# Graph layer with a selective-state scan: B rows by DMA broadcast, two banks as a ring for B and C, the next tile's gcn product in each tile's last step

## The chip, the cores and the metric

One core of a Trainium2 chip runs the whole program. The metric is the device time of one launch in microseconds (us), as the median over repeated runs; lower is better. The engines are named as in the profile: PE (TensorE, matrix products), DVE (VectorE), ACT (ScalarE), POOL (GpSimd), SP (the queue that only issues DMAs).

## What is computed

Two layers over a graph of 4096 nodes with 128 features. The first computes two branches `relu(...)` of `adj @ x` and `adj @ x2`, merges them, adds x and normalises each row. The second is the one that the change touches:

```
h = relu(adj @ x @ gcn_w + gcn_b); h = layernorm(h) * ln_g + ln_b
xc, z = split(h @ w_in); u = silu(causal_conv4(xc))
dt, B, C = split(u @ w_xp); dt = softplus(dt @ w_dt + b_dt)       # B, C: 16 values for each of 4096 steps
for t in 0..4095: s[d, n] = exp(dt[t, d] * A[d, n]) * s[d, n] + dt[t, d] * u[t, d] * B[t, n]
                  y[t, d] = sum_n s[d, n] * C[t, n]
out = layernorm(x + ((y + u * D_skip) * silu(z)) @ w_out)
```

with 256 channels d and 16 states n.

## The kernel before, in words

The first part of the program (up to about 480 us) is the first layer; it also writes the transposed matrix to DRAM (`adjT`). It isn't touched. The second part works on 8 tiles of 512 time steps. Each engine runs a function `window(b, ...)` for tile b, with one pass of a loop over steps n = 0..15 (plus one or two at its end) for the 16 states. What an engine does in a step is written out by hand, with the table `AT` (which step holds which piece), `PLAN` and `CONV` (how many products of 512 columns PE does in a step), and semaphores between engines.

For state n, with the channels on 128 partitions in 2 halves of 512 steps:

- PE spreads row n of B over all partitions: a product of `bc` with a selector column, into PSUM bank 6 (`spread_B`, line 1117). All 16 rows of B go through this one bank, so each waits until the one before it is consumed. The order is `SPREADS` (1, 0, 3, 2, ...), two steps ahead (`AHEAD`), each at the end of a step after the step's other work.
- For even n, DVE multiplies that bank with `dtu` into `dBuV` (line 887). For odd n, ACT copies the bank to SBUF (`copy_B`, line 655, tile `b_sb`), and POOL multiplies there into `dBuP` (line 480), not before DVE has scanned state n - 3.
- ACT computes `dA` (line 671). DVE scans (line 901, `hs`), one step later.
- PE spreads row n of C (`spread_C`, line 1127), at the end of step n + 1, into bank 5, or bank 4 for n = 1, 3, 5; each waits for the product before it in its bank. DVE multiplies `hs` with it into `pr` (line 908), in step n + 2. PE adds the product to y by 8 turning products (`sum_state`, line 1131), in step n + 3; those of states 14 and 15 (`LATE`) come in step 0 of the next window.

In between, window b does the front of tile b + 1 (`front_*`: gcn product on PE, line 1064; relu on ACT, line 590; statistics `front_g` on DVE, line 839; inverse deviation on POOL, line 450; convolution, z, B, C and dt products on PE; softplus on ACT, DVE line 857 and POOL lines 457, 462, 465), the tail of tile b - 1 (`tail_*`: gate, line 863; output product; statistics, line 869; POOL lines 470 and 472; `tail_norm` on ACT, line 713, in step 14), and for tile b + 2 the 32 blocks of `adj @ x` (`adj_blocks`, line 1052), which sum in bank 7.

These blocks read chunks of 4 blocks each. SP loads a chunk (1024 KB) from `adjT` into one of 4 buffers `adjc` (line 328). In SP's window stands in this order: the chunks 0 to 5 of tile b + 2, the store of tile b - 1's output (line 338), which waits for `tail_norm`, then chunks 6 and 7:

```
                load_res(b, par)
                if adj_:
                    load_adj(b + 2, range(0, CHUNKS - 2))
                if tail:
                    store(b - 1)
                if adj_:
                    load_adj(b + 2, range(CHUNKS - 2, CHUNKS))
```

The gcn product of tile b + 1 is PE's in step 0 of window b, after the sums of states 14 and 15, and ACT's copy of bank 7 for it (`front_ax`, line 585) in step 0 too. Windows 2 to 5 are a loop of two passes.

## Time and profile before

| | us |
|---|---|
| median of 3 runs | 1243.48 (1239.97 to 1245.7) |
| the profiled execution | 1238.24 |
| its span | 1236.7 |
| PE busy / DVE busy in the span | 1042.8 / 1056.5 |
| ACT busy / POOL busy | 543.7 / 325.3 |

The span is the time from the first to the last recorded instruction of the profiled execution; its own time stands 1.5 us above it. Busy time counts every record in full, so an engine that starts an instruction before the last one's record has ended (PE does, DVE a little) is less loaded than it looks. In the rows, `[0.61 <-PE bank L1117]` behind an instruction is its engine's idle time ahead of it and what ended that. State and step numbers are not in the rows: they follow from the order in the code.

### The profile page before, as it was taken

Reading aid. Unit: us, or ns where it says so; the run is one execution under the profiler, and the core shown is the slowest. Engines: PE = TensorE matmul, PEld = TensorE weight load, DVE = VectorE, ACT = ScalarE, POOL = GpSimd, SP = SyncE. Lnnn points to the kernel's source line nnn. Section 1 sums busy time; section 2 is a strip of 40 time slices with the busy share of each in tenths; the row PEclk is TensorE's granted clock in tenths of the full one; section 3 lists DMA queues with packets and bytes.
Section 4 is the critical chain, followed back from the end, with each engine's and each line's share of the span. In section 5 each row is a group of like instructions: output and inputs, shape, how many; then the busy total and the mean of one; then the engine's idle time right before and its main releaser. Section 6 shows DMA issues by size and latency. Waiting matters only on the chain. (4 is left out here: it accounts for less than half of the span.)

```text
span 1236.7 us, 13710 instructions
## 1 busy us (share of the span) xinstructions
PE 1042.8 (84%) x4306; PEld 709.1 (57%) x4306; DVE 1056.5 (85%) x864; ACT 543.7 (44%) x970; POOL 325.3 (26%) x208
## 2 busy tenths in 40 slices
PE   2789999999999999999888888888898888785555
PEld 1567677777777774445455555555455455453444
DVE  5899999999999996337878988978988879899994
ACT  2333333343333322145635546546457266455441
POOL 5100000101000011002262442622723624536330
PEclk9899999999999999999989999989999899896766
DMA  9999999999999998551321250520610511000000
GB/s 254 241 208 307 339 308 342 317 329 321 326 325 317 339 300 149 206 212 69 111 102 68 94 196 1 191 98 1 221 69 0 221 68 65 20 1 18 0 9 9
DMA packets 181948, 209.41 MB, mean 169 GB/s; under 512 B 7968, under 2 KB 163680, under 8 KB 167568
## 3 DMA queue, kind: packets, MB, share of 16 engines
q1 hardware_dynamic: 107008, 165.69, 41.8%
q10 hardware_dynamic: 71808, 35.66, 13.2%
q0 software_dynamic: 3088, 7.54, 2.2%
q8 instruction: 19, 0.31, 0.1%
q14 instruction: 25, 0.20, 0.1%
HBM read 145.94 MB, written 62.91 MB: 169 GB/s over the span
## 5 line engine op out<-in xcount | busy, mean ns | idle before, releaser
L760 DVE STREAM_TRANSPOSE at<-rows 128x1024 f32<-128x1024 f32 x136 | 267.3, 2006 | 26.4 <-DMA rows<-in_adj 16.0
L965 PE MATMUL yT<-ah,xh 128*128 128x512 f32 x512 | 214.4, 419 | 53.4 <-DVE al L768 53.4
L480 POOL TENSOR_TENSOR dBuP<-dtu,b_sb 128x1024 f32<-128x1024 f32 x64 | 165.9, 2592 | 268.7 <-DVE hs L901 211.8
L521 ACT ACTIVATE ah<-at 128x2048 fp32r<-128x2048 f32 x64 | 122.4, 1913 | 240.6 <-PE yT L965 229.4
L1052 PE MATMUL bank<-adjc,xm 128*128 128x512 f32 x448 | 219.0, 624 | 4.7 <-DMA adjc<-adjT 3.8
L965 PE MATMUL yT<-ah,xl 128*128 128x512 f32 x512 | 202.0, 395 | 0.0
L965 PE MATMUL yT<-al,xh 128*128 128x512 f32 x512 | 201.9, 394 | 0.0
L671 ACT ACTIVATE dA<-dt,A_sb 128x512 f32<-128x512 f32 x256 | 169.9, 715 | 47.4 <-POOL dt L462 45.2
L901 DVE TENSOR_TENSOR_SCAN hs<-dA,zero,dBuP 128x1026 f32<-128x1026 f32 x64 | 167.2, 2613 | 5.7 <-issue 4.5
L1131 PE MATMUL yT<-ident,pr 128*128 128x128 f32 x1024 | 152.0, 299 | 18.9 <-DVE pr L908 18.6
L908 DVE TENSOR_TENSOR pr<-hs,bank 128x1024 f32<-128x1024 f32 x128 | 153.0, 1196 | 9.7 <-PE bank L1127 9.7
L901 DVE TENSOR_TENSOR_SCAN hs<-dA,zero,dBuV 128x1026 f32<-128x1026 f32 x64 | 158.6, 2478 | 1.4 <-DVE dBuV L887 0.9
L1131 PEld LDWEIGHTS yT<-ident,pr 128*128 128x128 f32 x1024 | 134.7, 156 | 39.3 <-DVE pr L908 28.1
L965 PEld LDWEIGHTS yT<-ah,xh 128*128 128x128 f32 x512 | 97.6, 191 | 88.4 <-DVE al L768 64.9
L768 DVE TENSOR_TENSOR al<-at,ah 128x2048 fp32r<-128x2048 f32 x64 | 144.4, 2257 | 0.2
L1052 PEld LDWEIGHTS bank<-adjc,xm 128*128 128x128 f32 x448 | 84.6, 200 | 84.3 <-issue 77.3
L1127 PE MATMUL bank<-bc,sel 128*128 128x512 f32 x128 | 60.6, 473 | 77.6 <-DVE pr L908 77.5
L887 DVE TENSOR_TENSOR dBuV<-dtu,bank 128x1024 f32<-128x1024 f32 x64 | 78.0, 1218 | 50.1 <-PE bank L1117 47.3
L965 PEld LDWEIGHTS yT<-ah,xl 128*128 128x128 f32 x512 | 97.6, 191 | 23.8 <-issue 5.0
L965 PEld LDWEIGHTS yT<-al,xh 128*128 128x128 f32 x512 | 97.4, 190 | 21.3
L655 ACT ACTIVATE b_sb<-bank 128x512 f32<-128x512 f32 x64 | 38.0, 593 | 137.2 <-PE bank L1117 137.2
L1117 PE MATMUL bank<-bc,sel 128*128 128x512 f32 x128 | 90.2, 705 | 6.3 <-ACT b_sb L655 3.2
(148 smaller groups left out, 1048.5 us busy)
## 6 DMA issues: line engine op xcount, KB each, us to landing
adjT<-at SPq DMA_DIRECT2D x56, 1024.0 KB, 8.0
adjc<-adjT SPq DMA_DIRECT2D x56, 1024.0 KB, 5.1
rows<-in_adj SPq DMA_DIRECT2D x152, 256.0 KB, 8.6
rows<-in_adj ACTq DMA_DIRECT2D x136, 256.0 KB, 8.7
xm<-in_x SPq DMA_DIRECT2D x4, 512.0 KB, 16.2
xs<-in_L_gnn_x SPq DMA_DIRECT2D x4, 512.0 KB, 15.1
res<-in_x POOLq DMA_DIRECT2D x8, 256.0 KB, 7.5
mid<-xn POOLq DMA_DIRECT2D x8, 256.0 KB, 6.5
```

Of the source, the lines that this page charges most:

```text
L480: nc.gpsimd.tensor_tensor(dBu(n, par)[:, :, 1:], dtu[par][:, :, :], b_sb[pool_slot(n, par)][:, :].unsqueeze(1).to_broadcast([P, H, TILE]), ...
L521: nc.scalar.activation(ah[c % 2][:, :], at[c % 2][:, :, :].rearrange("p m t -> p (m t)"), ACT.Copy)\
L671: nc.scalar.activation(dA[n % NDA][:, h, 1:], dt_[par][:, h, :], ACT.Exp, scale=A_sb[:, h, n:n + 1]).then_inc(dA_ready, 1)
L760: last = nc.vector.transpose(dst.rearrange("p m (g i) -> p g m i", i=32), src.rearrange("p g (i m) -> p g m i", i=32))
L768: nc.vector.tensor_tensor(al[c % 2][:, :], at[c % 2][:, :, :].rearrange("p m t -> p (m t)"), ah[c % 2][:, :], ALU.subtract).then_inc(chunk ...
L887: nc.vector.tensor_tensor(dBuV[dve_slot(n, par)][:, :, 1:], dtu[par][:, :, :], BB[:, :].unsqueeze(1).to_broadcast([P, H, TILE]), ALU.mult)\
L901: nc.vector.tensor_tensor_scan(flat[0], flat[1], flat[2], zero[:, :], ALU.mult, ALU.add)\
L908: nc.vector.tensor_tensor(pr[k % NPR][:, :, :], hs[k % NHS][:, :, 1:], CC[k][:, :].unsqueeze(1).to_broadcast([P, H, TILE]), ALU.mult)\
L965: last = mm(acc[k][:, :], w[:, b, :], v[c % 2][:, cols], start=(b == 0 and j == 0), stop=(b == KB - 1 and j == 2))
L1052: last = mm(accB[:, :], xm[:, b, :], adjc[c % NADJ][:, m, :], start=(b == 0), stop=(b == KB - 1))
L1117: mm(BB[:, :], sel[:, n:n + 1].to_broadcast([P, P]), bc[par][:, :], start=True, stop=True).then_inc(B_spread, 1)
L1131: m = mm(yT[:, DI * q + P * h:DI * q + P * h + P], src[:, h, P * q:P * q + P], ident[:, :], is_transpose=True, start=first and h == 0 and ...
```

## The change

It does three things and moves a few others along.

1. The rows of B for the odd states (POOL's) no longer pass through PE's product and ACT's copy. After `bc` is made, ACT copies the 16 rows of B from PSUM to a small tile `b_rows`, and stores that to DRAM (`b_dram`, 32 KB). Two states at a time, it then issues a DMA which reads two rows and writes them to all 128 partitions (`load_B`, 512 KB, tiles `b_sb`): four such loads for a tile, in ACT's steps 14 (for the next tile), 2, 5 and 9. PE's dt product now also waits for `b_rows`, since it overwrites the bank.
2. Banks 5 and 6 form a ring. The 8 rows of B for even states and the 12 rows of C that aren't in bank 4 (now C of states 0, 2, 4, 6) take the two banks in turn, in the order of their use; each waits for the one two places before it. The row of B for state n + 1 is spread first thing in step n (n odd), row 0 of the next tile at the end of step 16.
3. The gcn product of tile b + 2 comes in the last step (16) of window b on PE, between the sum of state 13 and the spread of C for state 15; ACT's copy for it comes in step 15, the relu in step 0 of the next window. `PLAN` puts the 32 blocks on other steps.

SP's order, POOL's and DVE's are as before.

```diff
-          pe_z=7, pe_dbc=8, pe_dt=10, pe_turn=2, pe_out=9, act_B=-1, act_g=1, act_start=1, act_skip=2, act_y=4)
+          pe_z=7, pe_dbc=8, pe_dt=10, pe_turn=2, pe_out=9, act_b0=14, act_b1=2, act_b2=5, act_b3=9, act_ax=15, act_g=0, act_start=1, act_skip=2, act_y=4)
...
-PLAN = (1, 4, 3, 2, 0, 0, 1, 1, 1, 2, 0, 3, 3, 3, 4, 4)
-C_IN_O = (1, 3, 5)
+PLAN = (2, 4, 4, 1, 1, 0, 2, 1, 2, 1, 1, 3, 3, 2, 3, 2)
+C_IN_O = (0, 2, 4, 6)
...
+        ring = [it for n in range(S + 2) for it in (("B", n), ("C", n - 2))
+                if (it[0] == "B" and n < S and n not in POOL_B) or (it[0] == "C" and n >= 2 and n - 2 not in C_IN_O)]
+        def spread_bank(kind, n):
+            return bank[4] if kind == "C" and n in C_IN_O else bank[5 + ring.index((kind, n)) % 2]
...
                 nc.scalar.activation(bc[par][:, :], M0[:, :], ACT.Copy).then_inc(bcdt_high, 1)
+                nc.scalar.activation(b_rows[:, :], M0[0:S, :], ACT.Copy).then_inc(b_rows_ready, 1)
+                act.wait_ge(b_rows_ready, a + 1)
+                act.dma_start(b_dram[S * par:S * par + S, :], b_rows[:, :]).then_inc(b_stored, 16)
...
-            def copy_B(b, k, par):
-                act.wait_ge(B_spread, S * b + SPREADS.index(k) + 1)
-                wait(act, dBu_by_pool, NPB * b + nB(k) - 1)
-                nc.scalar.activation(b_sb[(nB(k) + NPB * par) % 2][:, :], BB[:, :], ACT.Copy).then_inc(B_copied, 1)
+            def load_B(b, par, pair):
+                if pair == 0:
+                    act.wait_ge(b_stored, 16 * (b + 1))
+                wait(act, dBu_by_pool, NPB * b + 2 * pair - 2)
+                rows_ = b_dram[S * par:S * par + S, :].rearrange("(k two) t -> two k t", two=2)[1]
+                act.dma_start(b_sb[pair % 2][:, :, :], rows_[2 * pair:2 * pair + 2, :].partition_broadcast(P))\
+                    .then_inc(b_in[pair % 2], 16)
...
+                    if n in (AT['act_b1'], AT['act_b2'], AT['act_b3']):
+                        load_B(b, par, 1 + (AT['act_b1'], AT['act_b2'], AT['act_b3']).index(n))
+                    if adj_ and n == AT['act_ax']:
+                        front_ax(b + 2)
                     if front:
-                        if n == (0 if tail else 1):
+                        if n == 1 and not tail:
                             front_ax(b + 1)
...
+                        if n == AT['act_b0']:
+                            load_B(b + 1, 1 - par, 0)
...
             def front_dtp(a, par):
                 pe.wait_ge(bcdt_low, a + 1)
+                pe.wait_ge(b_rows_ready, a + 1)
...
+            def bank_free(b, kind, n):
+                i = ring.index((kind, n))
+                (k, m), bb = (ring[i - 2], b) if i >= 2 else (ring[i - 2], b - 1)
+                if k == "B":
+                    wait(pe, dBu_by_dve, NVB * bb + m - nB(m) + 1)
+                else:
+                    wait(pe, C_multiplied, S * bb + m + 1)
...
             def window(b, par, tail, front, adj_):
                 for n in range(S + 1):
+                    if n % 2 and n + 1 < S:
+                        spread_B(b, n + 1, par)
                     if tail and n == 0:
                         for k in LATE:
                             sum_state(b - 1, k)
-                    if front and n == 0:
+                    if front and not tail and n == 0:
                         front_gcn(b + 1)
...
-                    if n + AHEAD < S:
-                        spread_B(b, n + AHEAD, par)
-                    elif front and n < S:
-                        spread_B(b + 1, n + AHEAD - S, 1 - par)
+                    if adj_ and n == S:
+                        front_gcn(b + 2)
                     if n > 0:
                         spread_C(b, n - 1, par)
+                    if front and n == S:
+                        spread_B(b + 1, 0, 1 - par)
```

Two places on PE show how the order moves. The first is where the blocks of chunk 6 begin (buffer `adjc2`, semaphore `adjT_in2`). Before, from the spread of C for state 11 (end of step 12) to the first block of chunk 6 in step 14; `pr2` and `pr3` hold the products of states 10 and 11:

```order
L1127 MATMUL bank5<-bc1,sel 128x512 [waits C_multiplied]
L1131 MATMUL yT<-ident,pr2 128x128 [waits C_multiplied]
L1131 MATMUL yT<-ident,pr2 128x128 x7
L1052 MATMUL bank7<-adjc1,xm 128x512 x3
L1114 REGISTER_ALU
L1117 MATMUL bank6<-bc1,sel 128x512 [waits B_copied]
L1122 REGISTER_ALU
L1127 MATMUL bank5<-bc1,sel 128x512 [waits C_multiplied]
L1131 MATMUL yT<-ident,pr3 128x128 [waits C_multiplied]
L1131 MATMUL yT<-ident,pr3 128x128 x7
L1052 MATMUL bank7<-adjc2,xm 128x512 [waits adjT_in2]
```

After, step 12 from the sum of state 9 (`pr1`), the spread of C for state 11 (into bank 5) and the start of step 13, with the spread of B for state 14:

```order
L1150 MATMUL yT<-ident,pr1 128x128 [waits C_multiplied]
L1150 MATMUL yT<-ident,pr1 128x128 x7
L1068 MATMUL bank7<-adjc1,xm 128x512 x2
L1068 MATMUL bank7<-adjc2,xm 128x512 [waits adjT_in2]
L35 REGISTER_ALU
L1146 MATMUL bank5<-bc1,sel 128x512 [waits dBu_by_dve]
L35 REGISTER_ALU
L1137 MATMUL bank6<-bc1,sel 128x512 [waits C_multiplied]
L1150 MATMUL yT<-ident,pr2 128x128 [waits C_multiplied]
```

The first block of chunk 6 now stands in step 12, ahead of the spread of C for state 11; before it stood two steps later, behind that spread and the next.

The second place is the end of a window. Before, from the spread of C for state 15 into the next window; `pr2` and `pr3` are states 14 and 15:

```order
L1127 MATMUL bank5<-bc1,sel 128x512 [waits C_multiplied]
L1234 REGISTER_ALU
L1234 COMPARE_AND_BRANCH
L1131 MATMUL yT<-ident,pr2 128x128 [waits C_multiplied]
L1131 MATMUL yT<-ident,pr2 128x128 x7
L1131 MATMUL yT<-ident,pr3 128x128 [waits C_multiplied]
L1131 MATMUL yT<-ident,pr3 128x128 x7
L1064 MATMUL bank2<-gcn_w_sb,axT 128x128 [waits sp_abs_relu,ax1_ready]
L1065 MATMUL bank2<-gcn_b_sb,ones 128x128
```

After, step 16 from the end of state 13's sum (`pr1`) to the spread of B for state 0 of the next tile (into bank 5):

```order
L1150 MATMUL yT<-ident,pr1 128x128 x7
L1080 MATMUL bank2<-gcn_w_sb,axT 128x128 [waits sp_abs_relu,ax1_ready]
L1081 MATMUL bank2<-gcn_b_sb,ones 128x128
L1080 MATMUL bank2<-gcn_w_sb,axT 128x128
L1081 MATMUL bank2<-gcn_b_sb,ones 128x128
L1080 MATMUL bank2<-gcn_w_sb,axT 128x128
L1081 MATMUL bank2<-gcn_b_sb,ones 128x128
L1080 MATMUL bank2<-gcn_w_sb,axT 128x128
L1081 MATMUL bank2<-gcn_b_sb,ones 128x128
L1146 MATMUL bank6<-bc1,sel 128x512 [waits C_multiplied]
L35 REGISTER_ALU [waits bcdt_low]
L1137 MATMUL bank5<-bc0,sel 128x512 [waits C_multiplied]
```

The 8 gcn products have moved from behind the sums of states 14 and 15 to ahead of the spread of C for state 15.

## Rows read from the trace of the kernel before

**Rows 1.** DVE's waits, 544 to 638 us (tile 0): waited for, us, times, longest.

```profile
DVE stats L839 <- ACT g L590: 13.6, 1, 13.6
DVE dBuV L887 <- PE bank L1117: 7.5, 4, 2.6
```

**Rows 2.** The same, 638 to 1068 us (tiles 1 to 5).

```profile
DVE dBuV L887 <- PE bank L1117: 35.2, 25, 3.3
DVE stats L839 <- ACT g L590: 8.8, 4, 2.7
DVE pr L908 <- PE bank L1127: 7.1, 9, 1.6
```

**Rows 3.** The same, 1068 to 1221 us (tiles 6 and 7).

```profile
DVE dBuV L887 <- PE bank L1117: 4.6, 4, 1.7
DVE pr L908 <- PE bank L1127: 1.8, 2, 0.9
DVE stats L839 <- ACT g L590: 1.4, 1, 1.4
```

**Rows 4.** PE: stretch, length, busy us, granted clock (1.00 is 2.4 GHz), DMA share, GB/s.

```profile
638.00:1068.00 430.00, 371.86 (x1590) 0.97 0.26 94
```

**Rows 5.** DVE's timeline in tile 2: start, us, instruction [idle before <-what ended it].

```profile
717.14 4.39 DVE L901 TENSOR_TENSOR_SCAN hs<-dA,zero,dBuP 128x1026 f32<-128x1026 f32 x1 [1.13 <-issue]
...
723.53 1.22 DVE L908 TENSOR_TENSOR pr<-hs,bank 128x1024 f32<-128x1024 f32 x1 [0.89 <-PE bank L1127]
...
734.51 1.22 DVE L887 TENSOR_TENSOR dBuV<-dtu,bank 128x1024 f32<-128x1024 f32 x1 [1.49 <-PE bank L1117]
```

**Rows 6.** POOL's timeline in tile 2.

```profile
733.29 2.38 POOL L480 TENSOR_TENSOR dBuP<-dtu,b_sb 128x1024 f32<-128x1024 f32 x1
741.45 2.40 POOL L480 TENSOR_TENSOR dBuP<-dtu,b_sb 128x1024 f32<-128x1024 f32 x1 [5.78 <-DVE hs L901]
```

**Rows 7.** DVE's timeline in tile 7: two scans, the second behind a `dBuV` without a wait.

```profile
1149.85 2.35 DVE L901 TENSOR_TENSOR_SCAN hs<-dA,zero,dBuV 128x1026 f32<-128x1026 f32 x1
...
1154.37 2.50 DVE L901 TENSOR_TENSOR_SCAN hs<-dA,zero,dBuP 128x1026 f32<-128x1026 f32 x1
```

**Rows 8.** All engines' timeline, 779 to 803 us (tile 2, steps 11 to 17).

```profile
787.77 0.88 SPq L328 DMA_DIRECT2D adjc<-adjT  x2
...
790.66 1.19 DVE L908 TENSOR_TENSOR pr<-hs,bank 128x1024 f32<-128x1024 f32 x1
...
792.24 1.03 PE L1131 MATMUL yT<-ident,pr 128*128 128x128 f32 x8
...
793.34 3.70 PE L1052 MATMUL bank<-adjc,xm 128*128 128x512 f32 x8
...
796.28 3.28 DVE L901 TENSOR_TENSOR_SCAN hs<-dA,zero,dBuV 128x1026 f32<-128x1026 f32 x1
```

**Rows 9.** PE's timeline at the start of tile 3: first of 8 gcn products, next block.

```profile
811.11 0.39 PE L1064 MATMUL bank<-gcn_w_sb,axT 128*128 128x128 f32 x2
...
814.33 1.97 PE L1052 MATMUL bank<-adjc,xm 128*128 128x512 f32 x2
```

**Rows 10.** PE's timeline where chunk 6 came late, then the clock behind it (stretch as in rows 4).

```profile
881.79 5.40 PE L1052 MATMUL bank<-adjc,xm 128*128 128x512 f32 x8 [1.86 <-DMA adjc<-adjT]
...
883.80:887.20 3.40, 3.40 (x7) 0.65 0.93 378
```

**Rows 11.** ACT's copies of B's rows in all, then its DMA issues in the first part.

```profile
L655 ACT ACTIVATE b_sb<-bank 128x512 f32<-128x512 f32 x64 | 38.0, 593 | 137.2 <-PE bank L1117 137.2
...
196.25 0.46 ACTq L281 DMA_DIRECT2D rows<-in_adj  x1
```

**Rows 12.** DMA issues: KB each, median us to landing; then `adjc` min/median/max.

```profile
xm<-in_x SPq DMA_DIRECT2D x4, 512.0 KB, 16.2
out<-o_n SPq DMA_DIRECT2D x8, 256.0 KB, 2.6
...
DMA to landing us min/median/max: 4.7/5.1/11.8
```

More of the change, by code:

```diff
@@ L159, in gnn_mamba @@
         y = sb("y", [P, H, TILE], F32, B)
-        b_sb = [sb(f"b_sb{k}", [P, TILE], F32, B) for k in range(2)]
+        b_sb = [sb(f"b_sb{k}", [P, 2, TILE], F32, B) for k in range(2)]
+        b_rows = sb("b_rows", [S, TILE], F32, B)
         o_n = sb("o_n", [P, RG, D], F32, B)
@@ L172, in gnn_mamba @@
         accB, M0, M1 = bank[7], bank[2], bank[3]
-        BB = bank[6]
-        CC = [bank[4] if n in C_IN_O else bank[5] for n in range(S)]
         O = bank[4][:, :].rearrange("p (g d) -> p g d", g=RG)
@@ L232, in gnn_mamba @@
         dtu_ready = sem("dtu_ready")
-        B_spread, C_spread, B_copied = sem("B_spread"), sem("C_spread"), sem("B_copied")
+        B_spread, C_spread = sem("B_spread"), sem("C_spread")
+        b_rows_ready, b_stored = sem("b_rows_ready"), sem("b_stored")
+        b_in = [sem(f"b_in{k}") for k in range(2)]
         dA_ready, start_set = sem("dA_ready"), sem("start_set")
@@ L882, in window @@
                     if n < S and n not in POOL_B:
[L883 removed]
+                        dve.wait_ge(B_spread, NVB * b + n - nB(n) + 1)
                         if n == 0:
@@ L1105, in front_dtp, with spread_B @@
                     mm(m[:, :], w_dtl[:, P * h:P * h + P], bc[par][:, :], start=False, stop=True).then_inc(dt_product, 1)
-            def spread_B(b, p, par):
-                n = SPREADS[p]
-                if p == 0:
-                    pe.wait_ge(bcdt_low, b + 1)
-                k, bb = (SPREADS[p - 1], b) if p else (SPREADS[-1], b - 1)
-                if not (isinstance(bb, int) and bb < 0):
-                    if k in POOL_B:
-                        pe.wait_ge(B_copied, NPB * bb + nB(k) + 1)
-                    else:
-                        pe.wait_ge(dBu_by_dve, NVB * bb + k - nB(k) + 1)
-                mm(BB[:, :], sel[:, n:n + 1].to_broadcast([P, P]), bc[par][:, :], start=True, stop=True).then_inc(B_spread, 1)
+            def bank_free(b, kind, n):
[5 more added lines that the diff above has]
+                    wait(pe, C_multiplied, S * bb + m + 1)
+            def spread_B(b, n, par):
+                if n == 0:
+                    pe.wait_ge(bcdt_low, b + 1)
+                bank_free(b, "B", n)
+                mm(spread_bank("B", n)[:, :], sel[:, n:n + 1].to_broadcast([P, P]), bc[par][:, :], start=True, stop=True).then_inc(B_spread, 1)
             def spread_C(b, n, par):
-                before = [k for k in range(n) if (k in C_IN_O) == (n in C_IN_O)]
-                if before:
-                    pe.wait_ge(C_multiplied, S * b + before[-1] + 1)
-                elif n in C_IN_O:
+                if n not in C_IN_O:
+                    bank_free(b, "C", n)
+                elif n == C_IN_O[0]:
                     wait(pe, o_normed, RG * (b - 1))
                 else:
-                    wait(pe, C_multiplied, S * b)
-                mm(CC[n][:, :], sel[:, S + n:S + n + 1].to_broadcast([P, P]), bc[par][:, :], start=True, stop=True).then_inc(C_spread, 1)
+                    pe.wait_ge(C_multiplied, S * b + C_IN_O[C_IN_O.index(n) - 1] + 1)
+                mm(spread_bank("C", n)[:, :], sel[:, S + n:S + n + 1].to_broadcast([P, P]), bc[par][:, :], start=True, stop=True).then_inc(C_spread, 1)
             def add_turned(src, h, first=False, last=False):
@@ L1226, in _ @@
             pe.wait_ge(selectors_ready, 4)
-            for p in range(AHEAD):
-                if p == 1:
-                    fill(7)
-                spread_B(0, p, 0)
+            spread_B(0, 0, 0)
+            fill(7)
             fill(8)
```

34 lines of the change are left out of this document (15 added, 19 removed).

## The prediction

> **What bounds the kernel now.** I read the waits of DVE first, because in the scan part it is the engine that everything else serves: 16 scans, 16 products with C and 8 with B in each tile, in a fixed order. In tile 0 it waits 13.6 us once for g, the input of the next tile's statistics, and 7.5 us for rows of B [rows 1]. In tiles 1 to 5 it waits 35.2 us for rows of B in 25 waits, five a tile, 8.8 us for g and 7.1 us for rows of C [rows 2]; in tiles 6 and 7, 4.6, 1.4 and 1.8 us [rows 3]. The waits for B are PE's order, not its load: PE is busy 372 of 430 us in tiles 1 to 5 at a granted clock of 0.97 [rows 4], but a row of B is issued at the end of a step, behind up to four blocks, and an even state's row can't be issued before the odd row ahead of it has been copied out of the one bank. So DVE's order plus these waits sets the time.
>
> The second thing to see is a loss that is no wait. A scan takes 2.35 us, but 4.39 us when POOL's product for `dtu` has just begun [rows 5, 7]. Both read two tensors from SBUF, and one stands until the other is through. At a tile's end POOL's softplus chain costs DVE 1.13 us of idle time ahead of scan 15, 2.04 us in it [rows 5] and 0.93 us in scan 14 (3.28 against 2.35) [rows 7, 8]: 4.1 us a tile.
>
> **What the change takes away.** B's row for each even state is now issued first thing in a step and needs only a bank that was used two items before, so I take all its waits off: 7.5 + 35.2 + 4.6 = 47.3 us [rows 1 to 3]. With the gcn product a step earlier, g is there before DVE asks: 8.8 + 1.4 = 10.2 us. Tile 0's 13.6 us stay, since that product hangs on the 32 blocks ahead of window 0, which aren't moved. Row 15 of C no longer waits for the product of state 14: 1.8 us in tiles 6 and 7, which have no gcn product at their end. Together 59.3 us.
>
> **What it gives back.**
>
> (a) The waits for B were cover. POOL's product for an odd state starts when DVE's scan ends and takes 2.4 us; DVE fills 2.25 us with a product with C and one with B, then wants to scan. Where no wait stands there now, that scan takes 2.50 us and not 2.35 [rows 7]. About 30 scans get this: 4.5 us.
>
> (b) POOL's product for state 3 comes after its work on the statistics and runs from 733.29 to 735.67 [rows 6]. DVE, without its 1.49 us wait [rows 5], would be at scan 1 1.5 us earlier, and stand until 735.6. So that wait only changes its name: 7 x 1.5 = 10.5 us.
>
> (c) The table for PE's blocks. Blocks 24 to 27 are chunk 6. They began in step 14 and now begin in step 12, ahead of the spread of C for state 11. But SP still issues that load behind the output's store, which waits for ACT's step 14; nothing of that chain is moved. In tile 2 the load was issued at 787.77, and PE began on it at 793.34, the moment it was there [rows 8]. DVE takes C for state 11 at 790.66. Now C comes one block (0.9 us) and one spread (0.4 us) behind the landing: at 794.6, a wait of 4.0 us, and I take 4.3 us, since part of it runs at the lower clock. While DVE stands, POOL works through its chain, so that of the 4.1 us above only some 1.3 us are left; PE, late by then, costs DVE some 0.6 us in steps 13 to 15. Net 4.3 - 2.8 + 0.6 = 2.1 us a tile, in the five tiles which have both a store and a chunk 6 (1 to 5): 10.5 us.
>
> (d) Step 16. After DVE's product of state 13, PE adds it (1.03 us [rows 8]), does 8 gcn products (814.33 - 811.11 = 3.2 us [rows 9]) and spreads C for 15 (0.4 us): 4.6 us. DVE has a scan and a product to do meanwhile, 2.35 + 1.19 = 3.5 us [rows 7, 8]. It waits at least 1.1 us, up to 3.0 if PE is a block or two behind; I take 2.0, where 0.89 was [rows 5]. Six tiles: 6.6 us.
>
> (e) ACT loses 64 copies of 0.59 us [rows 11] and gets per tile one copy and five DMA issues, of 0.46 us each by the one row for it [rows 11]. It isn't waited for now, so both are worth nothing, but 0.3 us ahead of window 0, where the copy and the issue stand in the chain. Without ACT's slack the issues would cost 2.3 us a tile.
>
> (f) The broadcast loads are in no row. From below: a 256 KB transfer lands in 2.6 us; from above: 512 KB took 16.2 us under full queues [rows 12]. The tightest is the load in ACT's step 2, which serves the product at 741.45 [rows 6]; ACT is at step 2 near scan 14 of the tile before, over 20 us ahead. I take nothing; the cover is POOL's distance.
>
> Given back: 4.5 + 10.5 + 10.5 + 6.6 + 0.3 = 32.4 us. Net 59.3 - 32.4 = 27 us. From the profiled execution, 1238.2, that gives 1211; that execution is 5 us below the median of the runs, 1243.5, and from the median the forecast is **1216 us**.
>
> **A rule against it.** ACT's queue is empty in this part before, so no row has two queues loading at once. In ACT's step 14 the first broadcast of the next tile is issued a few us ahead of chunk 6. The Trainium skill (DMA: Bandwidth & Descriptors, Issuing engines are not separate DMA queues) says that DMAs from different engines run on the same 16 DMA engines and interleave. By that rule the sum would be some 12 us smaller, 1229 us; by the rows alone it is 1216. It is the second rival, priced from rows there.
>
> **The rivals.**
>
> *The wait for chunk 6 is hidden (0.17).* If the load were there by 789.3, (c) falls away and the time is 1206. For it: DVE could lag for other reasons. Against: the load's issue hangs on DVE's own steps, so it moves along with DVE.
>
> *The broadcast delays chunk 6 (0.15).* 512 KB is half of a chunk, which takes 5.1 us to land [rows 12], so up to 2.5 us more, five times: 12.5 us, 1229. For it: the two are issued within 3 us. Against: the first should be nearly through when the second begins.
>
> *C for states 0 and 1 comes late (0.07).* Steps 1 and 2 have four blocks each (3.7 us) ahead of those spreads; at the lower clock they'd take twice that. 1.5 us in seven tiles: 1227. This is also the way in which the early rows of B would bring nothing: the wait moves on to C.
>
> *PE stays at half clock to the end of the tile (0.08).* PE comes to chunk 6 two steps earlier than now, where it comes just as the load lands, so it waits some 9 us. Behind a wait of 1.86 us eight instructions took 5.40 us, not 3.70, with the clock at 0.65 of its full rate over the next 3.4 us [rows 8, 10], that is at 1.2 GHz for most of it. If it stayed there over steps 13 to 16, four sums and seven blocks would take 4 x 1.03 + 7 x 0.9 = 10 us longer; half of it would reach DVE: 5 x 5 = 25 us, 1241: no change.
>
> *Slower: chunk 6 is really late (0.07).* Its slowest load landed after 11.8 us [rows 12]. If the landing is 11.8 and not 5.5 us in every tile, and the block behind it runs at half clock (0.9 us more), DVE loses 7.2 us more in five tiles: 36 us, 1252. It decides from 6.6 us more per tile on, (27 + 6.2) / 5.
>
> **How the numbers follow.** The forecast itself has 0.46. About 0.5% (6 us) is what a measurement of this kernel can tell from no change. Faster by more: forecast, first, second and third rival, 0.46 + 0.17 + 0.15 + 0.07 = 0.85; within: 0.08; slower: 0.07. The range goes from 1203 (the wait hidden and 3 us of (d) saved) to 1235 (the broadcast's delay together with 6 us for the upper end of (d)); it leaves out the last two rivals.
>
> **What would show it.** DVE has no wait for a row of B in tiles 1 to 6, and none for g but tile 0's. PE stands some 9 us in step 12 on a DMA of `adjc` in tiles 1 to 5, and DVE some 4 us at the product of state 11. DVE waits 1 to 3 us at the product of state 15 in tiles 0 to 5. Scans of odd states take 2.50 us, scan 1 about 3.8 us. From scan 0 to scan 0, tiles 1 to 5 take 81 to 83 us, against 86 on average (430 / 5). It is wrong if DVE is seen waiting for POOL's products on account of `b_sb`, if its waits for C in states 0 and 1 come to over 1 us a tile, or if tiles 1 to 5 aren't over 2 us shorter.

## The result, and the profile after

The changed kernel takes **1199.6 us** (median of 4 runs, 1197.6 to 1202.8) against 1244.6 us (1240.0 to 1246.5) for the kernel before on the same chip: a ratio of 0.965, 95% interval 0.961 to 0.968. The forecast was 1216 us, its range 1203 to 1235. The direction was right; the gain was larger than the whole range allowed. The profiled execution took 1201.0 us (span 1199.4), 37.3 us less than the one before (1238.2).

DVE's waits in tile 0 (544 to 632 us), to be held against [rows 1]:

```profile
DVE stats L855 <- ACT g L598: 10.5, 1, 10.5
DVE dBuV L903 <- PE bank L1137: 1.9, 1, 1.9
```

In tiles 1 to 5 (632 to 1037 us), against [rows 2]:

```profile
DVE pr L924 <- PE bank L1146: 32.8, 13, 5.9
DVE dBuV L903 <- issue: 2.0, 1, 2.0
```

The 25 waits for rows of B and those for g are gone; one idle time of 2.0 us ahead of a product with B is left, at the end of tile 3, which the profile puts down to "issue". Every kernel here has one there (1.2 to 2.6 us), where the loop over the windows turns; what it is was not tested. In their place stand waits of `pr`, DVE's product with C, for rows of C. Ten of the 13 make up nearly all: in each of tiles 1 to 5 one at the product of state 11 (4.94, 4.59, 4.40, 5.92, 4.15: 24.0 us) and one at that of state 15 (1.37, 1.38, 1.36, 2.14, 1.72: 8.0 us). All engines in tile 2, steps 11 to 17, against [rows 8, 9]:

```profile
762.80 0.37 ACTq L668 DMA_DIRECT2D b_sb<-b_dram  x1
...
767.05 0.88 SPq L335 DMA_DIRECT2D adjc<-adjT  x2
768.04 2.34 DVE L917 TENSOR_TENSOR_SCAN hs<-dA,zero,dBuV 128x1026 f32<-128x1026 f32 x1
...
772.44 2.08 PE L1068 MATMUL bank<-adjc,xm 128*128 128x512 f32 x2 [9.22 <-DMA adjc<-adjT]
...
773.52 1.42 PE L1146 MATMUL bank<-bc,sel 128*128 128x512 f32 x1
...
774.98 1.22 DVE L924 TENSOR_TENSOR pr<-hs,bank 128x1024 f32<-128x1024 f32 x1 [4.59 <-PE bank L1146]
...
777.25 4.48 DVE L917 TENSOR_TENSOR_SCAN hs<-dA,zero,dBuP 128x1026 f32<-128x1026 f32 x1
...
782.76 2.34 DVE L917 TENSOR_TENSOR_SCAN hs<-dA,zero,dBuV 128x1026 f32<-128x1026 f32 x1
...
787.20 0.39 PE L1080 MATMUL bank<-gcn_w_sb,axT 128*128 128x128 f32 x2
...
790.43 0.51 PE L1146 MATMUL bank<-bc,sel 128*128 128x512 f32 x1
...
790.97 1.22 DVE L924 TENSOR_TENSOR pr<-hs,bank 128x1024 f32<-128x1024 f32 x1 [1.38 <-PE bank L1146]
```

(A block stands in PE's rows as two records, so x2 is one block and x8 are four.) To be seen: chunk 6 is issued at 767.05, PE has stood 9.22 us for it when it lands, and then its first block takes 2.08 us, where [rows 8] had four in 3.70. C's spread for state 11, behind it, takes 1.42 us and is through at 774.94, 2.5 us after the landing, and DVE's product begins at 774.98. While DVE stood, POOL worked: `dtu`'s product is up against scan 13 (4.48 us), and scan 14 is a plain 2.34 where [rows 8] had 3.28. At the tile's end `C` for state 15 comes behind the eight gcn products, 1.38 us late.

Scan 1, and a plain and an odd scan behind it, from DVE's timeline of tile 2, against [rows 5, 7]:

```profile
718.88 3.67 DVE L917 TENSOR_TENSOR_SCAN hs<-dA,zero,dBuP 128x1026 f32<-128x1026 f32 x1
...
723.59 2.34 DVE L917 TENSOR_TENSOR_SCAN hs<-dA,zero,dBuV 128x1026 f32<-128x1026 f32 x1
...
728.09 2.45 DVE L917 TENSOR_TENSOR_SCAN hs<-dA,zero,dBuP 128x1026 f32<-128x1026 f32 x1
```

The page's DMA issues (KB each, median us to landing), against [rows 12]:

```profile
adjc<-adjT SPq DMA_DIRECT2D x56, 1024.0 KB, 5.3
...
b_sb<-b_dram ACTq DMA_DIRECT2D x32, 512.0 KB, 3.7
```

From scan 0 to scan 0 (tile 7: to its last scan's end), us, read from DVE's timeline; the last line is the kernel e2 below:

| tile | 0 | 1 | 2 | 3 | 4 | 5 | 6 | 7 |
|---|---|---|---|---|---|---|---|---|
| before | 94.8 | 87.2 | 84.4 | 89.6 | 81.4 | 86.7 | 81.7 | 66.1 |
| changed | 86.6 | 81.2 | 80.8 | 81.5 | 82.2 | 79.6 | 76.6 | 64.4 |
| e2 | 83.1 | 76.9 | 76.7 | 78.2 | 76.7 | 76.5 | 76.6 | 64.4 |

Tiles 1 to 5 take 81.1 us on average, inside the forecast's 81 to 83 (before: 85.9); tile 0 gave 8.2 us and tile 6 5.1. Tile 4 of the changed kernel is longer than before. The change carries a gain and a loss, and the second has the size of what is left to win.

### The profile page after: what moved, and what is told of

Its sections match the earlier page's. It is cut to its first block and busy times, and to the rows that moved or that the text cites. A ratio compares the mean times of both kernels' runs of the same rounds, so it can differ in the third digit from the quotient of the medians.

```text
span 1199.4 us, 13465 instructions
## 1 busy us (share of the span) xinstructions
PE 1021.9 (85%) x4242; PEld 706.7 (59%) x4242; DVE 1053.8 (88%) x864; ACT 515.4 (43%) x914; POOL 308.2 (26%) x208
## 3 DMA queue, kind: packets, MB, share of 16 engines
q10 hardware_dynamic: 80768, 52.70, 17.8%
## 5 line engine op out<-in xcount | busy, mean ns | idle before, releaser
L488 POOL TENSOR_TENSOR dBuP<-dtu,b_sb 128x1024 f32<-128x1024 f32 x64 | 155.9, 2436 | 265.7 <-DVE hs L917 210.5
L1150 PE MATMUL yT<-ident,pr 128*128 128x128 f32 x1024 | 158.5, 308 | 28.9 <-DVE pr L924 28.9
L1150 PEld LDWEIGHTS yT<-ident,pr 128*128 128x128 f32 x1024 | 139.0, 160 | 58.3 <-DVE pr L924 41.0
L917 DVE TENSOR_TENSOR_SCAN hs<-dA,zero,dBuP 128x1026 f32<-128x1026 f32 x64 | 170.5, 2664 | 2.6 <-ACT dA L683 2.6
L917 DVE TENSOR_TENSOR_SCAN hs<-dA,zero,dBuV 128x1026 f32<-128x1026 f32 x64 | 155.7, 2433 | 1.6 <-ACT dA L683 0.9
L1146 PE MATMUL bank<-bc,sel 128*128 128x512 f32 x128 | 89.9, 702 | 13.3 <-DVE pr L924 11.5
L676 ACT ACTIVATE state<-hs 128x2 f32<-128x2 f32 x128 | 25.7, 201 | 110.0 <-DVE hs L917 106.8
```

What stands on the lines that cost most here:

```text
L488: nc.gpsimd.tensor_tensor(dBu(n, par)[:, :, 1:], dtu[par][:, :, :], b_sb[pair % 2][:, nB(n) % 2:nB(n) % 2 + 1, :].to_broadcast([P, H, TILE ...
L917: nc.vector.tensor_tensor_scan(flat[0], flat[1], flat[2], zero[:, :], ALU.mult, ALU.add)\
L1146: mm(spread_bank("C", n)[:, :], sel[:, S + n:S + n + 1].to_broadcast([P, P]), bc[par][:, :], start=True, stop=True).then_inc(C_spread, 1)
L1150: m = mm(yT[:, DI * q + P * h:DI * q + P * h + P], src[:, h, P * q:P * q + P], ident[:, :], is_transpose=True, start=first and h == 0 and ...
```

## The experiments

The question after the result: which terms of the sum were mis-sized, and is what the table of blocks costs more than the forecast's 10.5 us? Twelve kernels ran. Median us, and ratio to the kernel before on the same chip with its interval:

| kernel | us | ratio |
|---|---|---|
| changed | 1199.6 | 0.965 (0.961 to 0.968) |
| e1 chunks 6, 7 ahead of the store | 1182.9 | 0.951 (0.945 to 0.957) |
| e2 old order of blocks | 1178.5 | 0.948 (0.942 to 0.954) |
| e3 C15, B0, gcn | 1225.3 | 0.985 (0.979 to 0.992) |
| e4 gcn back in step 0 | 1211.5 | 0.975 (0.967 to 0.983) |
| e5 e3 with relu in step 1 | 1222.9 | 0.978 (0.974 to 0.983) |
| e6 fixed banks | 1202.4 | 0.964 (0.961 to 0.968) |
| e7 gcn part alone | 1241.7 | 0.998 (0.994 to 1.002) |
| e8 broadcast and ring alone | 1201.0 | 0.963 (0.959 to 0.967) |
| e9 new order, chunks 6, 7 late | 1187.9 | 0.953 (0.949 to 0.957) |
| e10 C15, gcn, B0 | 1194.7 | 0.959 (0.954 to 0.963) |
| e11 e2 with 1/sigma later | 1177.1 | 0.944 (0.940 to 0.948) |
| e12 e9 with even steps 11 to 13 | 1178.7 | 0.950 (0.945 to 0.955) |

Where nothing else is said, the edit is made to the changed kernel. The twelve ran on four chips (e1 to e4, e5 to e8, e9 to e11, and e12), each beside the kernel before, whose median lay between 1242.0 and 1245.7 us. So differences of a few us between medians of different groups are not certain; where they carry an argument, the waits in the traces are given with them.

**e1: SP loads chunks 6 and 7 ahead of the store.**

```diff
-                    load_adj(b + 2, range(0, CHUNKS - 2))
+                    load_adj(b + 2, range(0, CHUNKS))
                 if tail:
                     store(b - 1)
-                if adj_:
-                    load_adj(b + 2, range(CHUNKS - 2, CHUNKS))
```

> The changed kernel, with SP's loads of chunks 6 and 7 issued ahead of the output's store. Theory (ledger of the two traces): PE's 9 us wait in step 12 goes, and with it DVE's waits at the product of state 11 (4.94, 4.59, 4.40, 5.92, 4.15 us, 24.0 in all); POOL's softplus chain costs its full 4.1 us per tile again where the trace has 1.4 now, so 10.5 us come back: 24.0 - 10.5 = 13.5 us less, about 1186 us. Rival (the wait is absorbed): DVE's lost time only changes its name, from the wait to POOL's chain and PE's load in steps 13 to 16, and the time stays within 3 us of 1200.

Measured 1182.9 us. DVE's waits for rows of C in the whole scan part come to 2.0 us in six waits. In tile 2 the chunk's blocks now start when their turn comes, with no wait for a transfer. The first row is step 12 with its three blocks, the last of them chunk 6's first; the second is step 13:

```profile
757.32 2.74 PE L1066 MATMUL bank<-adjc,xm 128*128 128x512 f32 x6
...
762.98 1.88 PE L1066 MATMUL bank<-adjc,xm 128*128 128x512 f32 x4
```

So the store ahead of the chunks is what holds them up. The waits at state 15 (8.0 us) went as well. The expectation came near by two errors: by its own figures POOL's chain would give back (4.1 - 1.4) x 5 = 13.5 us and leave 10.5, the other way round than it says, and it left the waits at state 15 out. The traces have 24.0 + 8.0 off, 7.9 back in the scans and 5.8 in idle time ahead of them: 18.3 us, of 17.8 between the two profiled executions.

**e2: the old order of blocks**, one line:

```diff
-PLAN = (2, 4, 4, 1, 1, 0, 2, 1, 2, 1, 1, 3, 3, 2, 3, 2)
+PLAN = (1, 4, 3, 2, 0, 0, 1, 1, 1, 2, 0, 3, 3, 3, 4, 4)
```

> The changed kernel with the old table of blocks (PLAN), so that chunk 6 begins in step 14 again. Theory: the wait for it goes as in the run before this, but steps 14 and 15 carry four blocks each ahead of C for 14 and the gcn product, so part returns as waits for C of states 14 and 15, 1 us more a tile: about 1192 us. Rival (absorbed): within 3 us of 1200. It also tells whether the table by itself was good: above 1200 it was.

Measured 1178.5 us, 13.5 below what I expected: I had thought that C for states 14 and 15 would come late behind the fuller last steps. DVE's longest waits in the scan part of this kernel are these; behind them come five rows of 2.6 us or less, and none of PE's rows for B or C is waited for at all:

```profile
DVE stats L855 <- ACT g L598: 9.5, 1, 9.5
DVE hs L917 <- issue: 6.8, 6, 1.1
DVE stats L885 <- PE bank L1183: 4.9, 1, 4.9
```

**e3: C for 15 and B for the next state 0 ahead of the gcn product.**

```diff
-                    if adj_ and n == S:
-                        front_gcn(b + 2)
                     if n > 0:
                         spread_C(b, n - 1, par)
                     if front and n == S:
                         spread_B(b + 1, 0, 1 - par)
+                    if adj_ and n == S:
+                        front_gcn(b + 2)
```

> The changed kernel, with the spreads of C for state 15 and B for state 0 ahead of the gcn product in step 16. Theory: DVE's waits at the product of state 15 (1.37, 1.38, 1.36, 2.14, 1.72 us, 8.0 in all) go, and g still comes before it is asked for: 8 us less, about 1192. Rival: PE has the same work to do in the same stretch, so the wait moves to the gate (sums of states 14 and 15) or to C of state 0 in the next tile, and the time changes by under 3 us.

Measured 1225.3 us: 26 slower in place of 8 faster. All engines at the end of tile 1 show a chain:

```profile
714.58 0.47 PE L1137 MATMUL bank<-bc,sel 128*128 128x512 f32 x1 [2.15 <-DVE pr L924]
...
718.50 0.80 PE L1080 MATMUL bank<-gcn_w_sb,axT 128*128 128x128 f32 x2
719.23 0.79 PE L1081 MATMUL bank<-gcn_b_sb,ones 1*128 1x128 f32 x2
...
720.14 0.60 ACT L598 ACTIVATE g<-bank 128x512 f32<-128x512 f32 x1 [7.64 <-PE bank L1081]
...
722.27 2.35 DVE L917 TENSOR_TENSOR_SCAN hs<-dA,zero,dBuV 128x1026 f32<-128x1026 f32 x1 [5.58 <-ACT state L676]
```

B's spread needs the bank in which C of state 14 lay, so it waits for that product; the gcn product stands behind it on PE, and after that wait six of its eight products take 0.80 us instead of 0.49; the relu waits for it on ACT; and behind the relu are the state copies and start values that scan 0 needs.

**e4: the gcn product, its copy and its relu where they were** (step 0 of the next tile, ACT's steps 0 and 1).

```diff
-                    if front and not tail and n == 0:
+                    if front and n == 0:
                         front_gcn(b + 1)
...
-                    if adj_ and n == S:
-                        front_gcn(b + 2)
...
-                    if adj_ and n == AT['act_ax']:
-                        front_ax(b + 2)
...
-                        if n == 1 and not tail:
+                        if n == (0 if tail else 1):
                             front_ax(b + 1)
```

and `act_g=1`.

> The changed kernel with the gcn product, ACT's copy for it and the relu back in their old places (step 0 and 1 of the next window); rows by DMA and the ring stay. Theory: DVE waits for g again, some 2 us a tile in tiles 1 to 6 as in the kernel before, and the row of B for state 2 is behind the product, so that the 1.3 us which scan 1 stands for POOL are covered by it; C of state 15 comes without a wait (8.0 us less). Sum: + 10 + 4 - 8, about 1206 us. Rival, that the early gcn product is what brought most of the gain: 1215 us or more.

Measured 1211.5 us (1206.2 to 1220.8), between theory and rival: this part is worth 12 us next to the new order of blocks. DVE waits 23.4 us for g, 10.1 of it in tile 0. The waits at state 15 went, as expected, but those at state 11 grew from 24.0 to 26.2 us, and short waits at states 1, 5 and 7 came.

**e5: e3 with the relu in step 1**:

```diff
-act_ax=15, act_g=0,
+act_ax=15, act_g=1,
```

> The kernel with C of state 15 and B of the next state 0 ahead of the gcn product (1225.3 us), with one thing more: ScalarE takes the relu of g in step 1, as before the change, and not in step 0. Theory: the 25 us that that kernel lost came from ScalarE's own queue, which stood in the relu in step 0 for the late gcn product while the copies of states 14 and 15 and the start values that VectorE's scans wait for were queued behind it. With the relu a step later these copies pass, the waits of 3 to 6 us of the first scans of a tile go, and the time is about 1200 us (1225 less some 25). Rival: TensorE's late product is itself what the tile waits for (g late at VectorE's statistics, all that follows late); then those waits only move there and the time stays above 1215 us.

Measured 1222.9 us: the rival held. Scan 0 of tile 2 no longer waits for ACT, but now g, the gate and the next row of B are late one after the other, each 1.4 to 1.7 us:

```profile
719.00 2.35 DVE L917 TENSOR_TENSOR_SCAN hs<-dA,zero,dBuV 128x1026 f32<-128x1026 f32 x1 [0.29 <-DVE dBuV L903]
...
723.01 0.87 DVE L855 BATCH_NORM_STATS2 stats<-g 128x6 f32<-128x128 f32 x4 [1.65 <-ACT g L598]
...
726.03 1.23 DVE L879 TENSOR_TENSOR yg<-yT,sz 128x1024 f32<-128x1024 f32 x1 [1.39 <-PE yT L1150]
...
728.76 1.22 DVE L903 TENSOR_TENSOR dBuV<-dtu,bank 128x1024 f32<-128x1024 f32 x1 [1.51 <-PE bank L1137]
```

The loss is PE's late product; ACT's queue only decided where DVE paid for it.

**e6: no ring**, B in bank 6 and C in bank 5 as before, each waiting for the last reader of its own bank:

```diff
-            return bank[4] if kind == "C" and n in C_IN_O else bank[5 + ring.index((kind, n)) % 2]
+            return bank[4] if kind == "C" and n in C_IN_O else bank[6 if kind == "B" else 5]
...
-                i = ring.index((kind, n))
-                (k, m), bb = (ring[i - 2], b) if i >= 2 else (ring[i - 2], b - 1)
+                own = [it for it in ring if it[0] == kind]
+                i = own.index((kind, n))
+                (k, m), bb = (own[i - 1], b) if i >= 1 else (own[-1], b - 1)
```

> The changed kernel without the ring: B's remaining spreads all go to bank 6, C's (outside the output's bank) all to bank 5. My prediction credited the ring with hardly anything but C of state 15 in time (1.8 us in tiles 6 and 7), since with GpSimd's states gone there is one B per two steps in its own bank. If so the time is 1200 to 1204 us. Rival: C of each state from 7 on then waits for the product of the state ahead, one bank for nine in a row, and comes late by the time from that product to the next one wherever TensorE is in blocks of the adjacency: 1 to 2 us in about five steps of seven tiles, so 1215 us or more. VectorE's waits at the products of states 8 to 15 tell.

Measured 1202.4 us, the same as with the ring by the intervals. The wait for chunk 6 sits in the trace as before, 4.1 to 4.5 us a tile; the waits at state 15 are 1.6 to 3.0 us there. In this kernel the ring is worth a few us at most; without the waits for chunk 6 it was not tried.

**e7: the gcn part alone, in the kernel before.** PE's part of the edit; ACT's is `front_ax` in step 15 and `act_g=0`, as in the change:

```diff
-                    if front and n == 0:
+                    if front and not tail and n == 0:
                         front_gcn(b + 1)
...
                     elif front and n < S:
                         spread_B(b + 1, n + AHEAD - S, 1 - par)
+                    if adj_ and n == S:
+                        front_gcn(b + 2)
                     if n > 0:
                         spread_C(b, n - 1, par)
```

> The kernel before with the third part alone: gcn product in the last step of a tile, the copy of the adjacency's sum in ScalarE's step 15, relu in step 0; B and C, their banks and the order of the blocks as before. Putting that part back cost 12 us in the changed kernel. Theory: the waits for g (10.2 us in tiles 1 to 7 of the profile) end here too, and C of state 15 comes up to 2 us later in six tiles, so about 1236 us. Rival: the product of state 0 or 1 then waits for B's copies, which are queued on ScalarE behind the relu, and takes the gain back: 1243 us or more.

Measured 1241.7 us, no change (0.994 to 1.002). Its longest waits in the scan part:

```profile
DVE pr L910 <- PE bank L1129: 34.7, 12, 6.6
DVE dBuV L889 <- PE bank L1119: 34.2, 29, 3.9
DVE stats L841 <- ACT g L590: 11.5, 1, 11.5
```

The waits for g are gone but for tile 0's, those for B fell from 47.3 to 34.2 us, and the waits for C rose from 9.7 to 34.7 us: at the product of state 15 up to 6.6. The gain was taken back in full; which of the rows ahead of C for 15 on PE does it in that kernel I did not separate.

**e8: broadcast and ring alone**, old order of blocks (as in e2), gcn part where it was: the diffs of e2 and e4 together.

> The first two parts of the change alone: DMA broadcast and the ring, with the old order of the adjacency's blocks and the gcn product, its copy and its relu where they were. If the parts add up, it is the kernel with the old blocks (1178.5 us) plus what the gcn product's move was worth in the changed kernel (11.9 us): 1190 us. If the gcn product's move is worth less where the last chunks are in time, it is nearer 1180 us; if the waits for g are longer here, 1195 us or more.

Measured 1201.0 us, where adding the parts gave 1190. Its waits for g (for rows of B and C it has none, like e2):

```profile
DVE stats L853 <- ACT g L598: 29.9, 7, 9.5
```

With e2 this says that moving the gcn product is worth 22 us beside the old order of blocks, 12 us beside the new one (e4) and at most a few us with B's rows still on PE and ACT (e7); and that the new order costs 11 us without that move and 21 us with it. The parts don't add up: each hides what another one left standing.

**e9: the new order with chunks 6 and 7 late.**

```diff
-PLAN = (2, 4, 4, 1, 1, 0, 2, 1, 2, 1, 1, 3, 3, 2, 3, 2)
+PLAN = (2, 4, 4, 1, 1, 0, 2, 1, 2, 1, 1, 3, 2, 0, 4, 4)
```

> The changed kernel with its order of blocks up to step 11, and only the last four steps altered, 2 0 4 4 instead of 3 2 3 2, so that the first block of chunk 6 stands in step 14 as in the old order and not in step 12. Putting the whole old order back took 21 us off (1178.5 us). Theory now: all of it hangs on the step of chunk 6's first block, whose transfer is issued behind the store of the last tile's output; the waits at the product of state 11 (24.0 us) and at that of state 15 (8.0 us), which I took for two different costs, are one. Then both go and the time is 1178 to 1184 us. Rival: the earlier blocks (ten in the first three steps) cost something of their own, and a part of the 21 us stays: 1190 us or more. Second rival: the waits of state 15 are from the gcn product ahead of C of state 15, as my prediction had it; then they stay, 8 us, and the time is about 1187 us.

Measured 1187.9 us, the price of the second rival. The waits at state 11 are gone, those at state 15 stay: 1.30, 1.53, 1.67, 1.99, 1.86. PE in tile 2: the stretch up to step 13's beginning and the one of step 13 (columns as in [rows 4], with PEld, DVE, ACT and POOL between), then the sum and the four blocks of step 14; last, the same four in e2:

```profile
761.00:766.00 5.00, 2.14 (x10) 1.63 (x9) 5.00 (x4) 4.35 (x14) 3.84 (x3) 0.80 0.49 160
766.00:771.40 5.40, 2.25 (x9) 2.06 (x10) 5.40 (x4) 0.00 (x0) 5.32 (x2) 0.50 1.03 371
```

```profile
769.75 1.91 PE L1150 MATMUL yT<-ident,pr 128*128 128x128 f32 x8
...
771.45 4.97 PE L1068 MATMUL bank<-adjc,xm 128*128 128x512 f32 x8
...
781.11 0.47 PE L1146 MATMUL bank<-bc,sel 128*128 128x512 f32 x1
...
782.29 0.39 PE L1080 MATMUL bank<-gcn_w_sb,axT 128*128 128x128 f32 x2
...
786.05 1.22 DVE L924 TENSOR_TENSOR pr<-hs,bank 128x1024 f32<-128x1024 f32 x1 [1.53 <-PE bank L1146]
```

```profile
764.08 3.60 PE L1068 MATMUL bank<-adjc,xm 128*128 128x512 f32 x8
```

PE stood 2.44 us for the bank of step 13's first row (761.05 to 763.49), and from 764.0 its granted clock was 0.50, the lower level. There was nothing for PE in step 13 but spreads and a sum, and the clock stayed down until 774.2. The blocks of step 14 ran 1.4 us longer for it, and the sum ahead of them, 1.91 us, 0.9 us longer than the 1.03 it has at the full clock.

**e10: C for 15, then the gcn product, then B for 0.**

```diff
-                    if adj_ and n == S:
-                        front_gcn(b + 2)
                     if n > 0:
                         spread_C(b, n - 1, par)
+                    if adj_ and n == S:
+                        front_gcn(b + 2)
                     if front and n == S:
                         spread_B(b + 1, 0, 1 - par)
```

> The changed kernel with C of state 15 ahead of the gcn product and B of the next state 0 still behind it (the kernel that lost 25 us had both ahead). If the waits at the product of state 15 (8.0 us in tiles 1 to 5) come from the gcn product ahead of C of state 15, as my prediction had it, they go and the time is about 1192 us. If they are the echo of chunk 6, they stay or move, and the time is about 1200 us. If the loss of 25 us came from C of state 15 ahead, and not from B of state 0 whose bank waits for the product of state 14, this kernel shows most of it: 1215 us or more.

Measured 1194.7 us. The waits at state 15 are gone (4.9 us off the changed kernel's median; 0.7 to 0.8 us came back per tile at state 0's row of B), those at state 11 remain. So the prediction's step (d) had the cause right: the gcn product ahead of C. And it is B's row ahead of the gcn product, not C's, that made e3 lose 26 us.

**e11: e2 with GpSimd's 1/sigma behind its product for state 3**:

```diff
-AT = dict(pool_rs=2,
+AT = dict(pool_rs=3,
```

> The best kernel so far (changed kernel with the old order of blocks, 1178.5 us), with one edit: GpSimd computes LayerNorm's 1/sigma of the next tile behind its product for state 3, not ahead of it. In six of its tiles scan 1 takes 3.67 instead of 2.35 us; it begins 0.85 us after that product (2.37 us) does and ends 2.35 us or so after it. Theory: the two cannot use their port at once, and the product stands so late only because 1/sigma waits for VectorE's statistics ahead of it. With the product at the end of scan 0 it runs beside VectorE's statistics and gating and is done when scan 1 begins: scan 1 is 2.35 us, up to 1.3 us per tile off, less what the gating (1.2 us) is stretched: 1170 to 1176 us. Rival: the product stretches the gating and the product of dBu by as much as it stretched the scan, or hn comes later by the 2.4 us and conv with it: 1178 us or above.

Measured 1177.1 us, 1.4 below e2: not to be told apart. Scan 1 did become a plain 2.35 us, but DVE's timeline in tile 3, and POOL's product beside it, show where most of the time went:

```profile
783.80 0.84 DVE L855 BATCH_NORM_STATS2 stats<-g 128x6 f32<-128x128 f32 x4
...
785.15 1.20 DVE L863 TENSOR_SCALAR mr<-mv 128x4 f32<-128x4 f32 x1
786.26 0.15 DVE L864 TENSOR_SCALAR ve<-mv 128x4 f32<-128x4 f32 x1
786.34 1.21 DVE L879 TENSOR_TENSOR yg<-yT,sz 128x1024 f32<-128x1024 f32 x1
...
788.60 2.35 DVE L917 TENSOR_TENSOR_SCAN hs<-dA,zero,dBuP 128x1026 f32<-128x1026 f32 x1
```

```profile
783.96 2.36 POOL L488 TENSOR_TENSOR dBuP<-dtu,b_sb 128x1024 f32<-128x1024 f32 x1 [3.63 <-DVE hs L917]
```

An instruction on four elements per partition, 0.17 us elsewhere, stood until POOL's product ended at 786.3. Of 1.33 us saved, 1.03 were paid there.

**e12: e9 with steps 11 to 13 filled evenly.**

```diff
-PLAN = (2, 4, 4, 1, 1, 0, 2, 1, 2, 1, 1, 3, 2, 0, 4, 4)
+PLAN = (2, 4, 4, 1, 1, 0, 2, 1, 2, 1, 1, 1, 1, 3, 4, 4)
```

> The kernel with the new order of blocks up to step 11 and the chunks late (1187.9 us), with the six blocks before chunk 6 spread 1 1 3 over steps 11 to 13 where they stood 3 2 0. There TensorE had nothing but small work in step 13, its granted clock fell to 0.50 and the eight blocks of step 14 took 4.97 us in place of 3.60, so that C of state 14, the gcn product and C of state 15 behind it were late by that: waits of 1.3 to 2.0 us at the product of state 15 in tiles 1 to 5, 8.4 us. Theory: they are that lateness passed through the gcn product, which leaves C of state 15 no slack; with the clock up they go and the time is about 1180 us. Rival: the early blocks of the new order hold TensorE back by themselves; the waits stay and the time is 1186 us or more.

Measured 1178.7 us: the waits at state 15 are gone. PE's clock fell here too, at 760.2 in tile 2, within 2.88 us in which PE stood for a bank, but it was back at the full level 3.4 us later, and step 14's blocks took 3.70 us. The medians of e9 and e12 are 9.2 us apart; their ratios to the kernel before, on two chips, are not clear of each other (0.949 to 0.957, 0.945 to 0.955), so the case rests on the 8.4 us of waits that are in one trace and not in the other. The new order's early blocks cost nothing that matters; what costs is chunk 6 in step 12, and a step without blocks ahead of the tile's end. The lateness of C for 15 thus needs both, the gcn product ahead of it and a PE that is behind.

e2 and e12 (and e11, no different) beat the changed kernel by 21 us in their medians (18 to 25 by the ratios) and the kernel before by 5%.

## Why the prediction was wrong

The time came out 3.4 us below the range, and the direction and the waits as forecast: no waits for B in tiles 1 to 6 (but the 2.0 us put down to issue), g waited for in tile 0 alone, PE 9 us and DVE 4 to 6 us on chunk 6, waits of 1.4 to 2.1 us at state 15 in tiles 1 to 5. The sizes of the terms did not hold, and one term, the copy ahead of g in tile 0, was put at nothing and wasn't nothing. By the two profiled executions, in us (scans: what the 128 scans take beyond 2.35 each, 25.2 in all before and 25.3 after):

| step | forecast | measured | from |
|---|---|---|---|
| waits for B | +47.3 | +46.0 | 49.9 (2.6 of it put down to issue), now 3.9 |
| waits for g | +10.2 | +13.3 | 23.8, now 10.5 |
| C but for state 11: 1.8 off, (d) on | -4.8 | -0.2 | 9.7, now 9.9 |
| (a) scans 2 to 12 | -4.5 | -2.0 | 1.6, now 3.6 |
| (b) scan 1 | -10.5 | -5.6 | 2.9, now 8.5 |
| (c) chunk 6 | -10.5 | -13.7 | wait 24.0, less 7.5 (scans 13 to 15) and 2.8 (idle ahead of scans) |
| (e), and the end | -0.3 | -1.7 | DVE's last waits, 8.3, now 10.0 |
| sum | 26.9 | 36.1 | of 37.3 |

**(b) was the largest miss: 4.9 us.** I took it that the 1.5 us wait of tile 2 stood ahead of scan 1 in all of seven tiles and would turn into standing. Scan 1 stands 1.33 us, in six tiles; and in tiles 4 and 6 of the kernel before it stood already, 1.1 and 1.3 us, which I hadn't looked up (tile 6):

```profile
1075.69 3.67 DVE L901 TENSOR_TENSOR_SCAN hs<-dA,zero,dBuP 128x1026 f32<-128x1026 f32 x1
```

A value seen in one tile was multiplied by seven.

**(d), 4.6 us, was right in cause and wrong in what it replaces.** "I take 2.0, where 0.89 was ... Six tiles." The waits at state 15 were 1.6 us in five tiles. And 0.89 was one tile's value; [rows 2] had 7.1 us for C in tiles 1 to 5, 1.4 a tile, all of which went. A wait that replaces another must be set against the row of its whole group.

**g in tile 0, 3.1 us, was written off.** "That product hangs on the 32 blocks ahead of window 0" is half of it. All engines in tile 0 of the kernel before:

```profile
556.49 0.79 PE L1065 MATMUL bank<-gcn_b_sb,ones 1*128 1x128 f32 x2
...
558.30 1.42 PE L1117 MATMUL bank<-bc,sel 128*128 128x512 f32 x1
...
559.75 0.60 ACT L655 ACTIVATE b_sb<-bank 128x512 f32<-128x512 f32 x1 [5.53 <-PE bank L1117]
560.24 0.59 ACT L590 ACTIVATE g<-bank 128x512 f32<-128x512 f32 x1
560.87 0.87 DVE L839 BATCH_NORM_STATS2 stats<-g 128x6 f32<-128x128 f32 x4 [13.59 <-ACT g L590]
```

The gcn product was ready at 557.3, and the relu stood for 3 us behind a copy of B's row, on ACT's queue, whose spread stood behind PE's blocks. The change takes that copy away: (e) says "It isn't waited for now, so both are worth nothing", and that is the step that failed. A copy that is only 0.6 us long was in the way for its wait, not for its length. e8, with the broadcast and the ring alone, already has tile 0's wait at 9.5 us; e7, which keeps the copy and moves the gcn product of the other tiles, has it at 11.5. Part of the wait is PE's clock: in the kernel before and in the changed one it fell to the lower level within this gcn product (at 555.1 and 555.6), in e7 and e8 it stayed at the full one. Before against changed and e7 against e8, at like clocks, the waits are 3.1 and 2.0 us apart.

**(a), 2.5 us.** Three odd scans a tile take 2.45, the others 2.35; I had reckoned with four or five at 2.50.

**(c), 3.2 us the other way.** The wait was 4.8 us on average and not 4.3, since C came 2.5 us behind the landing and not 1.3: behind 9.2 us of idle time PE's block took 2.08 us and not 0.9, and C's spread 1.42 and not 0.4 (their records overlap). What POOL's chain gives back was sized rightly against e2 (scans 13 to 15 there 14.8 us in tiles 1 to 5, 6.8 in the changed kernel, and 5.6 of idle time: 13.6 of 24.0; the forecast had 14.0), but the kernel before had some of that already, so that against it only 10.3 came back. The 3.0 us that I had added for a late PE in steps 13 to 15 are no row of their own; what there is of them lies in the waits at state 15, under (d).

**The two profiled executions.** The one before lies 6.4 us below its median, the one after 1.3 above. I took the first into account only by subtracting from the median a gain sized on it. The medians are 45.0 apart, the executions 37.3; that gap of 7.7 alone would have left the result inside the range (1216 - 7.7 = 1208). With the 9.2 us by which the steps' sum fell short it came out 3.4 us below it.

**The rivals.** The wait for chunk 6 wasn't hidden (first). That the broadcast delays chunk 6 (second) didn't happen: `adjc` lands in 5.3 us by the median, 5.1 before, and of the 9.22 us of PE's wait 3.8 passed before the load was issued, behind the store, and 5.4 from there to the landing. The load in ACT's step 14 was issued at 762.80, lands in 3.7 by the median, and chunk 6 was issued at 767.05, so the two hardly met; the Trainium skill's rule of interleaving engines (DMA: Bandwidth & Descriptors, Issuing engines are not separate DMA queues) is not put to the test by it. C for states 0 and 1 wasn't late but for 0.2 us in tile 0 (third). PE's clock had fallen while it stood for the chunk, stayed at the lower level for 2.9 to 5.0 us behind the landing (to 777.4 in tile 2), and then came back (fourth). The fifth did not occur: the longest wait was 5.9.

## What to carry to other kernels

Where several waits stand in the way of one engine, the parts of a change don't add up: the same move of the gcn product was worth next to nothing, 12 and 22 us, as the waits behind it were still there or not. Size what a new wait replaces by the whole group's row, and look tile by tile before a value is multiplied. And when work is pulled forward in one queue, follow the transfer that feeds it: here the blocks moved two steps ahead and their load stayed behind a store, and two loads in another place on SP's queue, or one line of the table, were worth 17 to 21 us.

## What I had not expected of the hardware

A `TENSOR_SCALAR` of 128x4 on DVE took 1.20 us instead of 0.17 beside POOL's product (e11), while `BATCH_NORM_STATS2`, a copy, an aggregate and, in e2, a `TENSOR_TENSOR` with one operand in PSUM kept their times beside it. The Trainium skill (SBUF — State Buffer, Who interferes with whom) names `tensor_scalar` among the operations that can take the port shared with GpSimd, under conditions on its operands; this row agrees, and shows that four elements a partition are no protection. The page names `copy` as well; the copy of one element here kept its 0.15 us, and no run varies the operands.

In e9, a kernel whose PE is busy 86% of the span, PE's clock was at the lower level from 764.0 to 774.2 us in tile 2: it fell behind a stand of 2.44 us and lasted through a step of 5.4 us in which PE was busy 2.25. In e12, with three blocks in that step, the low stretch was 3.4 us. The longer one cost 2.3 us in a sum and four blocks and, through the queue behind them, the waits of 8.4 us (1.3 to 2.0 a tile) that e12 doesn't have. The two kernels differ only in where six blocks stand in steps 11 to 13.

The broadcast of 512 KB to 128 partitions landed in 3.7 us by the median, less than a fourth of the 16.2 us of [rows 12]'s upper bound, and issuing it cost ACT 0.37 us where I had taken 0.46.
